# Two wide attention layers: queries projected for three batches at once, and softmax reciprocals spread over partitions by transfers

## The chip, the cores and the metric

The kernel runs on one core of a Trainium2 chip. The metric is the device time of one execution in microseconds (us). Three runs of the kernel before took 2034.56, 2040.13 and 2043.69 us, median 2040.13.

## What is computed

Four cross-attention layers follow one another. All have 16 batches, 100 queries and 361 context rows of width 256, and 16 heads. Layers L0 (with a feed-forward part) and L3 have heads of 16 and are "narrow"; L1 and L2 have heads of 64, so that their projections are 1024 wide, and are "wide". The change touches only the wide ones:

```python
# L1: x -> x + softmax(q k^T) v @ wo
normed = x * rsqrt(mean(x**2, -1) + 1e-6) * norm_w
q, k, v = heads(normed @ wq), heads(ctx @ wk), heads(ctx @ wv)      # 16 heads of 64
x = x + merge(softmax(q @ k.T) @ v) @ wo
# L2: rope on q and k, a key mask, and a layer norm behind the sum
q, k, v = rope(heads(x @ Wq)) / 8, rope(heads(ctx @ Wk)), heads(ctx @ Wv)
s = where(mask, q @ k.T, -1e9)
x = layer_norm(x + merge(softmax(s) @ v) @ Wo, 1e-3) * gamma + beta
```

## The kernel before

Everything is float32. A product that has to be exact enough is made of three float32r matmuls: both factors are split into a high and a low part, and high x high, high x low and low x high are added in PSUM (`product3`, L1358). ACT makes the high part, DVE (or POOL) the low part; so each product of 256 rows is six matmuls and is then taken out of PSUM twice.

`wide_layers` (L1170) runs L1 and L2 as one stream of 32 steps s: 0 to 15 are the batches of L1, 16 to 31 those of L2 ("rope" is `s >= B`). A step has four quarters d, and each quarter treats two head pairs, p = 2d and 2d + 1. The order of PE in a quarter is written out by hand (L1465 and on): the scores of both pairs; `weigh`, the probabilities times V, of the two pairs of the quarter before; the jobs called first (two key products K for the next step); `turn`, six transposes of the probabilities of the first pair; the jobs called mid (values V, the output projection O, and R, below); `turn` of the second pair; the jobs called late (a query product Q, and X). `jobs_at` (L1221) hands the jobs out. All jobs share three PSUM banks in turn: a job waits until the one three places back has been taken out (`begin`).

The scores of a pair lie in two banks. Of the pair that comes first in a quarter DVE copies the turned probabilities out (L1723), of the second ACT does (`unload`, L1591); the second pair's scores of the next quarter wait for that.

Queries: Q(s, p) is the product for head pair p of two batches, s and s + 1, so of 200 columns. X(s) transposes the two batches of x, normed in L1, as input. Step s even makes Q(s + 2, 4 to 7) and step s odd Q(s + 1, 0 to 3), one in each quarter; the tiles QH and QL have 12 places, of which pairs 4 to 7 use two in turn (`q_slot`). In L2 a key or query product also needs rope: DVE shuffles it into SH (L1679), ACT copies it to T32 (L1516), POOL multiplies both by the tables (L1928, L1929), in the next quarter DVE adds them into AC (`join`, L1684), ACT rounds AC to the high part (L1524), and the low part is made by DVE for keys (L1690) and by POOL for queries (L1935), for POOL behind the rotations of that quarter's keys. SH and AC are rings of four, T32 of three. POOL also makes masked tables for the next step at d = 0 (L1909 to L1913).

Reciprocals: the weighed values lie in PSUM with the head's dimension on the partitions and the queries on the columns, but the sums of the exponentials lie with the queries on the partitions. For each half batch (s, r), r = 0 at d = 2 and r = 1 at d = 0 of the next step, DVE takes the reciprocals of eight heads (L1728) and repeats each 64 times into RX (L1732). PE transposes RX in four pieces (job R, L1405), ACT copies the result from PSUM to RB (L1549), and DVE multiplies the weighed values by RB (`scale`, L1739), and later splits off the output's low part (L1744). `weigh` of the next half, at d = 1 for r = 1, waits for `scaled`.

SyncE (SP) issues the transfers of the wide layers in one order: the turned context of each step into the one tile C as soon as DVE has split the one before (L1666, at d = 3), masks, and weights.

Of the kernel before, what the change touches and what calls it, by code (L numbers as in the profile page):

```python
# [4 lines left out]
fp32 = mybir.dt.float32  # L5
# [7 lines left out]
KE = E // 128  # L13
# [23 lines left out]
def build(nc, a, consts, out):  # L37
    stack = ExitStack()
    with stack:
# [30 lines left out]
        strips_dram = nc.dram_tensor("strips", (2, 4, 32, 4, SKE), fp32, kind="Internal").ap()  # L70
        kept_dram = nc.dram_tensor("kept", (B, 2, 128, KE, SK), fp32, kind="Internal").ap()
# [1098 lines left out]
        def wide_layers():  # L1170
# [10 lines left out]
                  "inverse", "repeated", "spread", "scaled", "added", "o_high", "o_low", "wo_high", "wo_low",  # L1181
# [4 lines left out]
            wo2_in = sem("wide_wo2_in")  # L1186
            RAW2 = {"Q": 0, "K": 0, "V": 1}
# [10 lines left out]
            QH, QL = local("QH", [128, 12, 2 * SQ], f32r), local("QL", [128, 12, 2 * SQ], f32r)  # L1198
# [7 lines left out]
            XN = local("XN", [SQ, 2, E])  # L1206
            XTH, XTL = local("XTH", [128, KE, 2 * SQ], f32r), local("XTL", [128, KE, 2 * SQ], f32r)
# [12 lines left out]

            def jobs_at(s, d):  # L1221
# [25 lines left out]
            FIRST = [("K", 0, p) for p in range(4)] + [("X", 0, 0)] + [("K", 0, p) for p in range(4, HP)] + [("Q", 0, p) for p in (4, 5, 6, 7, 0, 1, 2, 3)] + [("X", 2, 0)] + [("V", 0, c) for c in range(3)]  # L1247
# [5 lines left out]
            CHUNKS = [(0, "K", 0, 256), (0, "K", 256, 512), (0, "K", 512, 1024), (0, "Q", 512, 1024), (0, "Q", 0, 512), (0, "V", 0, 512), (0, "V", 512, 1024),  # L1253
                      (1, "Q", 512, 1024), (1, "Q", 0, 512), (1, "K", 0, 256), (1, "K", 256, 512), (1, "V", 0, 512), (1, "K", 512, 768), (1, "K", 768, 1024),
                      (1, "V", 512, 1024)]
            CHUNKS_AT = {(13, 0): [7], (14, 0): [8], (14, 3): [9], (15, 0): [10], (15, 1): [11, 12], (15, 2): [13], (15, 3): [14]}
            CHUNK_AFTER = {7: ("Q", 14, 7), 8: ("Q", 14, 3), 9: ("K", 15, 7), 10: ("K", 15, 7), 11: ("V", 15, 2), 12: ("K", 15, 7), 13: ("K", 15, 7),
                           14: ("V", 15, 5)}

            def q_slot(s, p):  # L1260
                return 4 + p if p >= 4 and s // 2 % 2 else p

            def q_no(s, p):
                return HP * (s // 2) + (p + 4) % 8 + 1
# [32 lines left out]
            def taken(key):  # L1297
                kind, s, n = key
                if kind in "KQ" and rope(s):
                    return Z["copied"], turn_no[key] + 1  # L1300
                return {"K": lambda: (Z["k_low"], HP * s + n + 1), "Q": lambda: (Z["q_low"], q_no(s, n)),
                        "X": lambda: (Z["x_low"], s // 2 + 1), "V": lambda: (Z["v_taken"], 6 * s + n + 1),
                        "R": lambda: (Z["spread"], 2 * s + n + 1), "O": lambda: (Z["added"], s + 1)}[kind]()
# [4 lines left out]
            with nc.Block() as block:  # L1308

                @block.sync  # L1310
                def _(sp):
# [11 lines left out]
                    mask(B + 1)  # L1323
                    for s in range(NS):
                        if s + 1 < NS:
                            sp.wait_ge(Z["c_low"], KE * (s + 1))
                            load_turned_context(sp, s + 1)
                        if s == 0:
# [709 lines left out]
```

## Time and profile before

| | |
|---|---|
| median of 3 runs | 2040.13 us |
| profiled execution | 2039.82 us, span 2038.0 us |
| PE busy | 1936.0 us, 95% |
| DVE busy | 1433.7 us, 70% |
| ACT busy | 1312.6 us, 64% |
| POOL busy | 642.4 us, 32% |
| wide layers | about 455 to 1708 us of the span |

Times are microseconds. PE is TensorE, DVE VectorE, ACT ScalarE, POOL GpSimd. A row of the timeline is: start in the span, duration of the whole group, engine, line, operation, tiles as out<-in, form, how many instructions, and, where the engine was idle before, how long and for whom it waited. Durations of matmuls overlap, as they are pipelined; the difference of two starts is what a piece of work costs PE.

### The profile page before, as it was taken

The numbers are of one execution on the slowest core, as the hardware profiler recorded it, in microseconds if no ns is written. First come the engines' busy times: TensorE is split into PE (matmuls) and PEld (weight loads), VectorE is DVE, ScalarE is ACT, GpSimd is POOL, SyncE is SP. The second block draws the span as 40 slices with busy tenths as digits, with TensorE's granted clock in tenths as the row PEclk, the third lists the DMA queues.
The fourth block names the chain that finished last, engine by engine and source line by source line (L and its number), as shares of the span: only waits on it lengthen the run. The fifth ranks groups of instructions, "written<-read, shape, count | busy, mean of one in ns | idle before, by whom it ended". The sixth has DMA issues, their size and how long they took to land. (4 is left out here: it accounts for less than half of the span.)

```text
span 2038.0 us, 51007 instructions
## 1 busy us (share of the span) xinstructions
PE 1936.0 (95%) x19166; PEld 1683.5 (83%) x19166; DVE 1433.7 (70%) x2779; ACT 1312.6 (64%) x3193; POOL 642.4 (32%) x740
## 2 busy tenths in 40 slices
PE   7799998899999999999999999999999999899998
PEld 6677777898888888888888888888888878787786
DVE  5687786546555555555588888888888885677675
ACT  4576776556656566566576666666666763677775
POOL 3232330000000000000067777877877851000000
PEclk8899999999999999999999999999999998999999
DMA  5444442201000000000001000000000001344442
GB/s 154 150 140 137 134 135 68 91 26 57 14 8 16 9 9 16 9 9 16 29 10 53 11 10 10 18 10 10 17 11 10 9 1 64 119 123 125 129 121 66
DMA packets 72859, 109.65 MB, mean 54 GB/s; under 512 B 7052, under 2 KB 62508, under 8 KB 72620
## 3 DMA queue, kind: packets, MB, share of 16 engines
q1 hardware_dynamic: 72332, 105.88, 17.1%
q8 instruction: 158, 2.59, 0.5%
q14 instruction: 81, 0.66, 0.1%
q10 hardware_dynamic: 288, 0.51, 0.1%
HBM read 69.18 MB, written 37.19 MB: 52 GB/s over the span
## 5 line engine op out<-in xcount | busy, mean ns | idle before, releaser
L1584 ACT ACTIVATE wide_P<-PS,MX 100x361 f32<-100x361 f32 x512 | 280.9, 562 | 126.7 <-DVE MX L1717 126.3
L644 ACT ACTIVATE L_P<-PS,MX 100x361 f32<-100x361 f32 x512 | 252.7, 565 | 129.2 <-DVE MX L774 127.4
L774 DVE TENSOR_REDUCE MX<-PS 100x2 f32<-100x722 f32 x256 | 219.8, 900 | 55.1 <-PE PS L524 54.9
L1717 DVE TENSOR_REDUCE MX<-PS 100x2 f32<-100x722 f32 x256 | 221.2, 900 | 20.2 <-PE PS L1432 19.4
L536 PE MATMUL PP<-CON,L_P 100*128 100x100 f32 x1536 | 181.6, 255 | 27.6 <-DVE L_PT L781 23.1
L536 PEld LDWEIGHTS PP<-CON,L_P 100*128 100x128 f32 x1536 | 149.2, 143 | 48.8 <-ACT L_P L644 34.8
L1439 PE MATMUL PS<-CON,wide_P 100*128 100x100 f32 x1536 | 176.0, 249 | 1.1 <-ACT wide_P L1584 0.6
L1439 PEld LDWEIGHTS PS<-CON,wide_P 100*128 100x128 f32 x1536 | 157.5, 140 | 20.0 <-ACT wide_P L1584 3.1
L1928 POOL TENSOR_TENSOR wide_AC<-wide_T,wide_COSM 128x362 f32<-128x362 f32 x128 | 130.7, 1021 | 125.3 <-ACT wide_T L1516 119.9
L1452 PEld LDWEIGHTS PP<-wide_PT,wide_V 128*64 128x64 f32 (+1 forms) x3072 | 136.1, 136 | 33.1 <-issue 33.1
L1452 PE MATMUL PP<-wide_PT,wide_V 128*64 128x100 f32 (+1 forms) x3072 | 161.2, 253 | 0.6 <-issue 0.5
L1541 ACT ACTIVATE wide_V<-PJ 128x512 f32<-128x512 f32 (+1 forms) x129 | 76.3, 595 | 121.6 <-PE PJ L1358 121.4
L1888 POOL TENSOR_TENSOR VE<-MV 128x2 f32<-128x2 f32 x8 | 1.7, 218 | 477.9 <-DVE MV L1780 477.9
L1929 POOL TENSOR_TENSOR wide_SH<-wide_SH,wide_SINM 128x362 f32<-128x362 f32 x128 | 138.3, 1080 | 0.0
L1358 PE MATMUL PJ<-wide_CTH,wide_WH 128*128 128x362 f32 x338 | 120.0, 355 | 1.9 <-DVE wide_WL L1661 1.0
L1690 DVE TENSOR_TENSOR wide_KL<-wide_AC,wide_KH 128x362 fp32r<-128x362 f32 x128 | 114.2, 932 | 0.0
L1358 PE MATMUL PJ<-wide_CTH,wide_WL 128*128 128x362 f32 x338 | 111.1, 329 | 0.0
L1358 PE MATMUL PJ<-wide_CTL,wide_WH 128*128 128x362 f32 x338 | 111.1, 329 | 0.0
L1358 PE MATMUL PJ<-wide_WH,wide_CTH 128*128 128x512 f32 (+1 forms) x258 | 108.3, 420 | 0.0
L781 DVE COPY L_PT<-PP 128x600 f32<-128x600 f32 x128 | 99.4, 777 | 8.6 <-PE PP L536 3.8
L1584 ACT ACTIVATION_READ_ACCUMULATOR wide_P<-PS,MX 100x1 f32 x512 | 103.7, 203 | 0.0
L1516 ACT ACTIVATE wide_T<-PJ 128x362 f32<-128x362 f32 (+1 forms) x128 | 54.6, 427 | 74.7 <-DVE wide_SH L1679 72.8
(258 smaller groups left out, 5720.2 us busy)
## 6 DMA issues: line engine op xcount, KB each, us to landing
strips<-L_KS SPq DMA_DIRECT2D x256, 90.5 KB
L_KA<-strips SPq DMA_DIRECT2D x64, 362.0 KB, 3.2
C<-ctx_t SPq DMA_DIRECT2D x32, 361.0 KB, 3.1
kept<-L_CTH SPq DMA_DIRECT2D x16, 361.0 KB, 4.7
kept<-L_CTL SPq DMA_DIRECT2D x16, 361.0 KB, 5.3
L_CTH<-kept SPq DMA_DIRECT2D x16, 361.0 KB, 4.2
L_CTL<-kept SPq DMA_DIRECT2D x16, 361.0 KB, 5.0
C<-in_ctx SPq DMA_DIRECT2D x8, 256.0 KB, 3.5
```

The lines of the kernel that those rows point to most:

```text
L536: last = nc.tensor.transpose(PPB[:, n, SQ * t:SQ * t + SQ], P[:, (4 * g + 2 * i + n) % 8, 128 * t:128 * t + 128], ident[0:SQ, 0:SQ])
L644: nc.scalar.activation(P[:, (4 * g + j) % 8, 0:SK], PSB[0:SQ, j, 0:SK], ACT.Exp, bias=MX[:, s % 2, 4 * q + j:4 * q + j + 1], scale=1.0).th ...
L774: nc.vector.tensor_reduce(MX[:, s % 2, 4 * q + 2 * i:4 * q + 2 * i + 2], PSB[0:SQ, 2 * i:2 * i + 2, 0:SK], AX.X, ALU.max, negate=True).the ...
L781: nc.vector.tensor_copy(pt(g)[:, 2 * KV_TILES * SQ:4 * KV_TILES * SQ].rearrange("p (n c) -> p n c", n=2), PPB[:, :, 0:KV_TILES * SQ]).then ...
L1358: last = nc.tensor.matmul(dst, l, r, start=n == 0, stop=n == len(todo) - 1)
L1439: last = nc.tensor.transpose(score_bank(g, i)[:, SQ * t:SQ * t + SQ], P[:, (2 * g + i) % 4, 128 * t:128 * t + 128], ident[0:SQ, 0:SQ])
L1452: last = nc.tensor.matmul(PO[64 * i:64 * i + 64, SQ * at:SQ * at + SQ], V[0:r, 1024 * c + 64 * h:1024 * c + 64 * h + 64], PT[0:r, (2 * g + ...
L1584: nc.scalar.activation(P[:, (2 * g + i) % 4, 0:SK], score_bank(g, i)[0:SQ, 0:SK], ACT.Exp, bias=MX[:, s % 2, h:h + 1], scale=1.0, accum_ou ...
L1690: nc.vector.tensor_tensor(KL[:, p, :], AC[:, r % NB, 0:SKE], KH[:, p, :].bitcast(fp32), ALU.subtract).then_inc(Z["k_low"], 1)
L1717: nc.vector.tensor_reduce(MX[:, s % 2, 2 * p:2 * p + 2], PSB[0:SQ, 2 * (g % 2):2 * (g % 2) + 2, 0:SK], AX.X, ALU.max, negate=True).then_in ...
L1928: nc.gpsimd.tensor_tensor(ac, src, c, ALU.mult)
L1929: nc.gpsimd.tensor_tensor(sh, sh, t, ALU.mult).then_inc(Z["rotated"], 1)
```

## The change

Queries are made for groups: batches (0, 1), (2, 3), (4 to 6), (7 to 9), (10 to 12), (13 to 15) of each layer. A product has 200 or 300 columns, and QH and QL have 8 places with no second one. Q(s0, 0) to Q(s0, 4) are made in the step before the group, one, two, one and one in its quarters, behind the scores that last read the place; Q(s0, 5), Q(s0, 6) at (s0, 0) and Q(s0, 7) at (s0, 1). X is a job for each half of the width, both at d = 3 two steps ahead.

The job R, the tile RX and ACT's copy to RB are gone. DVE takes the reciprocals at d = 1 and d = 3 into RD, transposes it in 32 x 32 blocks into RT, and SP writes RT to a scratch tensor in HBM with four transfers, waits for them, and reads it back into RB with two transfers that repeat each row over 64 partitions. `scale` stays where it was and waits for these. SP's order is now written by quarters, with these steps at d = 1 and 3, at d = 3 behind the context's load. The diff, cut to its core:

```diff
-            QH, QL = local("QH", [128, 12, 2 * SQ], f32r), local("QL", [128, 12, 2 * SQ], f32r)
+            QH, QL = local("QH", [128, 8, 3 * SQ], f32r), local("QL", [128, 8, 3 * SQ], f32r)
-            RX = local("RX", [SQ, H // 2 * 64])
+            RD, RT = local("RD", [128, 32]), local("RT", [128, 32])
...
+            GROUPS = {s0 + l: n for l in (0, B) for s0, n in ((0, 2), (2, 2), (4, 3), (7, 3), (10, 3), (13, 3))}
+            Q_AHEAD, Q_WITHIN = {0: (0,), 1: (1, 2), 2: (3,), 3: (4,)}, {0: (5, 6), 1: (7,)}
...
             def jobs_at(s, d):
-                if s % 2 == 0 and s + 2 < NS:
-                    late.append(("Q", s + 2, 4 + d))
-                if s % 2 and s + 1 < NS:
-                    late.append(("Q", s + 1, d))
-                if s % 2 and d == 3 and s + 3 < NS:
-                    late.append(("X", s + 3, 0))
+                if s + 1 in GROUPS:
+                    late += [("Q", s + 1, p) for p in Q_AHEAD[d]]
+                if s in GROUPS and s > 0:
+                    late += [("Q", s, p) for p in Q_WITHIN.get(d, ())]
+                if d == 3 and s + 2 in GROUPS:
+                    late += [("X", s + 2, k) for k in range(KE)]
-                if d == 0 and s > 0:
-                    mid.append(("R", s - 1, 1))
-                if d == 2 and s < NS:
-                    mid.append(("R", s, 0))
...
                 @block.sync
+                    def reciprocals(s, r):
+                        n = 2 * s + r
+                        sp.wait_ge(Z["inverse_turned"], n + 1)
+                        for b in range(4):
+                            sp.dma_start(recip_dram[n % 2, :, 32 * b:32 * b + 32], RT[32 * b:32 * b + H // 2, :]).then_inc(recip_out, 16)
+                        sp.wait_ge(recip_out, 64 * (n + 1))
+                        if n:
+                            sp.wait_ge(Z["o_low"], n)
+                        for i in range(2):
+                            src = recip_dram[n % 2].rearrange("(t i) q -> i t q", i=2)[i:i + 1, :, 0:SQ]
+                            sp.dma_start(RB[64 * i:64 * i + 64, :, :], src.broadcast_to([64, 4, SQ])).then_inc(recip_in, 16)
...
                     for s in range(NS):
+                        for d in range(4):
...
+                            if d == 3 and s + 3 < NS:
+                                context(s + 3)
+                            if d in (1, 3):
+                                reciprocals(s, d // 2)
...
                 @block.vector
                     def invert(s, r):
                         n = 2 * s + r
                         dve.wait_ge(Z["exped"], HP * (n + 1))
-                        nc.vector.reciprocal(RDEN[:, 0:8], DEN[:, s % 2, 8 * r:8 * r + 8]).then_inc(Z["inverse"], 1)
+                        nc.vector.reciprocal(RD[0:SQ, 0:8], DEN[:, s % 2, 8 * r:8 * r + 8]).then_inc(Z["inverse"], 1)
                         dve.wait_ge(Z["inverse"], n + 1)
                         if n:
-                            dve.wait_ge(Z["made"], job_no["R", (n - 1) // 2, (n - 1) % 2] + 1)
-                        nc.vector.tensor_copy(RX[:, :].rearrange("p (h r) -> p h r", h=H // 2),
-                                              RDEN[:, 0:8].unsqueeze(2).to_broadcast([SQ, H // 2, 64])).then_inc(Z["repeated"], 1)
+                            dve.wait_ge(recip_in, 32 * n)
+                        nc.vector.transpose(RT[:, :], RD[:, :]).then_inc(Z["inverse_turned"], 1)

                     def scale(s, r):
-                        dve.wait_ge(Z["spread"], 2 * s + r + 1)
+                        dve.wait_ge(recip_in, 32 * (2 * s + r + 1))
                         dve.wait_ge(Z["weighed"], HP * s + 4 * r + 4)
...
                     for s, d in SLOTS:
-                        if d == 0 and s:
-                            invert(s - 1, 1)
-                        if d == 2 and s < NS:
-                            invert(s, 0)
                         for key in turns_of(G - 1):
                             join(key)
...
                         for key in turns_of(G - 1):
                             if key[0] == "K":
                                 rotated_low(key)
+                        if d in (1, 3) and s < NS:
+                            invert(s, d // 2)
```

The rest of the diff puts the new counts and column widths into the waits, the instructions for x's moments and POOL's power (three columns, not two), and the order of the first weights.

## Rows read from the trace of the kernel before

**Rows 1.** The page's busy tenths of PE in 40 slices of the span.
```profile
PE   7799998899999999999999999999999999899998
```
**Rows 2.** Timeline, PE: first scores of (1, 0), (15, 0), (16, 0), (30, 0).
```profile
509.55 0.41 PE L1432 MATMUL PS<-wide_KH,wide_QH 64*100 64x362 f32 x2
...
1029.91 0.41 PE L1432 MATMUL PS<-wide_KH,wide_QH 64*100 64x362 f32 x2
...
1069.06 0.41 PE L1429 MATMUL PS<-wide_MNEG,wide_FILL 64*100 64x362 f32 x2
...
1630.87 0.41 PE L1429 MATMUL PS<-wide_MNEG,wide_FILL 64*100 64x362 f32 x2
```
**Rows 3.** Timeline, PE, end of (11, 2): job R, turn, query product; then (11, 3)'s scores.
```profile
907.47 0.51 PE L1405 MATMUL PJ<-CON,wide_RX 100*128 100x100 f32 x4
907.82 0.68 PE L1439 MATMUL PS<-CON,wide_P 100*128 100x100 f32 x6
908.28 0.34 PE L1358 MATMUL PP<-wide_XTH,wide_WH 128*128 128x200 f32 x1
...
909.11 0.41 PE L1432 MATMUL PS<-wide_KH,wide_QH 64*100 64x362 f32 x2
...
909.68 0.33 PE L1432 MATMUL PS<-wide_KH,wide_QH 64*100 64x362 f32 x2
```
**Rows 4.** Groups by line and form, PE: count, busy us, mean ns, idle.
```profile
L1358 PE MATMUL PJ<-wide_CTH,wide_WL 128*128 128x362 f32 x338 | 111.1, 329 | 0.0
...
L1358 PE MATMUL PJ<-wide_WOH,wide_OTL 128*100 128x256 f32 x184 | 51.6, 280 | 0.0
...
L1358 PE MATMUL PJ<-wide_XTH,wide_WL 128*128 128x200 f32 x174 | 47.7, 274 | 0.0
```
**Rows 5.** Timeline, PE and ACT, from (31, 2) to (31, 3), without query products.
```profile
1691.69 0.68 PE L1439 MATMUL PS<-CON,wide_P 100*128 100x100 f32 x6
...
1692.30 0.41 PE L1429 MATMUL PS<-wide_MNEG,wide_FILL 64*100 64x362 f32 x2
1692.43 0.68 ACT L1591 ACTIVATE wide_PT<-PS 128x600 f32<-128x600 f32 x1
...
1693.35 0.41 PE L1429 MATMUL PS<-wide_MNEG,wide_FILL 64*100 64x362 f32 x2 [0.15 <-issue]
```
**Rows 6.** Timeline, PE: scores of (22, 0), (22, 1) first and second, (22, 3).
```profile
1311.12 0.41 PE L1429 MATMUL PS<-wide_MNEG,wide_FILL 64*100 64x362 f32 x2
...
1322.65 0.41 PE L1429 MATMUL PS<-wide_MNEG,wide_FILL 64*100 64x362 f32 x2
...
1324.07 0.41 PE L1429 MATMUL PS<-wide_MNEG,wide_FILL 64*100 64x362 f32 x2 [0.51 <-issue]
...
1342.62 0.41 PE L1429 MATMUL PS<-wide_MNEG,wide_FILL 64*100 64x362 f32 x2
```
**Rows 7.** Timeline, DVE's context split in L1 and L2, POOL's low parts of queries.
```profile
915.39 0.97 DVE L1666 TENSOR_TENSOR wide_CTL<-C,wide_CTH 128x361 fp32r<-128x361 f32 x2
...
1310.15 2.50 DVE L1666 TENSOR_TENSOR wide_CTL<-C,wide_CTH 128x361 fp32r<-128x361 f32 x2
...
1323.44 0.53 POOL L1935 TENSOR_TENSOR wide_QL<-wide_AC,wide_QH 128x200 fp32r<-128x200 f32 x1
...
1344.56 0.53 POOL L1935 TENSOR_TENSOR wide_QL<-wide_AC,wide_QH 128x200 fp32r<-128x200 f32 x1
```
**Rows 8.** Timeline, SP, in L3; then transfers: KB each, median us to landing.
```profile
1734.12 2.14 SPq L302 DMA_DIRECT2D strips<-L_KS  x4
1740.80 0.33 SPq L307 DMA_DIRECT2D L_KA<-strips  x1
...
wide_M<-in_mask SPq DMA_DIRECT2D x16, 45.1 KB, 2.8
```
**Rows 9.** Timeline, DVE, end of L2: last copy to RX and last scale.
```profile
1697.07 0.43 DVE L1732 COPY wide_RX<-RDEN 100x512 f32<-100x512 f32 x1
...
1699.66 0.57 DVE L1739 TENSOR_TENSOR wide_RB<-PP,wide_RB 128x400 f32<-128x400 f32 x1 [2.16 <-ACT wide_RB L1549]
```

More of the change, by code:

```diff
@@ L1218, in rope @@
                 return s >= B
+            GROUPS = {s0 + l: n for l in (0, B) for s0, n in ((0, 2), (2, 2), (4, 3), (7, 3), (10, 3), (13, 3))}
+            STARTS = list(GROUPS)
+            START_OF = {s0 + u: s0 for s0, n in GROUPS.items() for u in range(n)}
+            Q_AHEAD, Q_WITHIN = {0: (0,), 1: (1, 2), 2: (3,), 3: (4,)}, {0: (5, 6), 1: (7,)}
             def jobs_at(s, d):
@@ new lines, in _ @@
+                    context(1)
+                    sp.wait_ge(Z["w_low"], 7)
+                    for m in "QV":
+                        weights(m)
+                    context(2)
+                    for s in range(NS):
+                        for d in range(4):
+                            if (s, d) == (B - 2, 1):
+                                sp.wait_ge(Z["w_low"], 9)
+                                weights("K")
+                            if d == 0 and rope(s) and s + 2 < NS:
+                                sp.wait_ge(Z["m_tables"], s - B + 1)
+                                mask(s + 2)
+                            if (s, d) == (B, 0):
+                                sp.wait_ge(Z["w_low"], len(CHUNKS))
+                                load_weights(sp, "L3")
+                            if (s, d) == (B, 2):
+                                sp.wait_ge(Z["added"], B)
+                                sp.dma_start(WO[:, :].rearrange("p (t n) -> p t n", t=8),
+                                             a["L2_xattn_Wo"].rearrange("(t p) n -> p t n", p=128)).then_inc(wo2_in, 16)
+                            if d == 3 and s + 3 < NS:
+                                context(s + 3)
+                            if d in (1, 3):
+                                reciprocals(s, d // 2)
@@ L1414, in job @@
                     def job(key):
-                        {"K": keys, "V": values, "X": query_turn, "Q": queries, "R": spread, "O": project}[key[0]](key)
+                        {"K": keys, "V": values, "X": query_turn, "Q": queries, "O": project}[key[0]](key)
                     def scores(s, p):
@@ L1431, in scores @@
                             for n, r in halves:
-                                last = nc.tensor.matmul(score_bank(g, n)[0:SQ, 0:SKE], Q_[r, q_slot(s, p), q], K_[r, p, :], start=m == 0 and not rope(s), stop=m == 2)
+                                last = nc.tensor.matmul(score_bank(g, n)[0:SQ, 0:SKE], Q_[r, p, q], K_[r, p, :], start=m == 0 and not rope(s), stop=m == 2)
                         last.then_inc(Z["scored"], 1)
@@ L1542, in values @@
                                              ACT.Copy).then_inc(Z["v_taken"], 1)
-                    def spread(key):
-                        _, s, r = key
-                        act.wait_ge(Z["made"], job_no[key] + 1)
-                        if 2 * s + r:
-                            act.wait_ge(Z["o_low"], 2 * s + r)
-                        nc.scalar.activation(RB[:, :, :].rearrange("p t q -> p (t q)"), bank(key)[:, 0:4 * SQ], ACT.Copy).then_inc(Z["spread"], 1)
                     def output_high(s, r):
```

195 lines of the change are left out of this document (84 added, 111 removed).

## The prediction

> **What bounds the kernel now.** The page's slices show PE busy in nine tenths or more almost throughout; the last slices on the list are a second narrow layer that the change leaves alone [rows 1]. Busy time of pipelined matmuls hides short waits, so I read the wide layers from the starts of PE's instructions. One batch has four quarters (s, d), each of which begins with the scores of a head pair. From (1, 0) to (15, 0), in the plain layer L1, 14 batches take 520.4 us, 37.17 each; from (16, 0) to (30, 0), in the rope layer L2, 561.8 us, 40.13 each [rows 2]. L2's scores have one more step of two matmuls, the mask; one step is a third of 0.57 us [rows 3], and eight pairs make 1.5 us. That leaves 40.13 - 37.17 - 1.5 = 1.45 us of waits in each rope batch, 20 us over 14. In L1 nothing on PE waits: its time is the sum of its starts. So each start of a PE instruction that goes is worth its full price in L1, and in L2 if no wait takes its place.
>
> **The transposes that spread the reciprocals.** One such job begins at 907.47 and the next work at 907.82 [rows 3]: 0.35 us. There are 64, two in each of 32 batches: -22.4 us. With them go an eviction on ACT and a 100x512 copy of 0.43 us on DVE [rows 9]; neither is on PE's path in L1.
>
> **The query products.** A product of 200 columns takes from 908.28 to 909.11, 0.83 us [rows 3]. The means of one matmul are 274 ns at 200 columns, 280 at 256, 329 at 362 [rows 4]; on the line between the last two 300 columns give 300 ns, 26 more, and six make 0.16: 0.99 us for a product of three batches (bounds: 0.87 by the row of 256, 1.25 if it grew with the columns). Before, each of the 120 quarters of batches 0 to 29 has one product: 99.6 us. After, 88 are left there (24 of 200 columns, 64 of 300): 24 x 0.83 + 64 x 0.99 = 83.3, and 22 of them directly follow another and save an end of some 0.1: 81 us. But 54 quarters now have none. What these cost can be seen at the end of L2, where no queries are left: from the last transposes to the scores it is 0.61 us, not 0.46, and the second score waits until 1.05 us after the first, because ACT's unload of the bank (1692.43) was covered by the product [rows 5]. Normal is 0.57 in L1 and 0.57 + 0.19 in L2 [rows 3]. So a bare quarter costs 0.15 + 0.48 in L1 (24 of them) and 0.15 + 0.3 in L2 (19); 11 more have the transposes of x, which cover the unload: 0.15. Together 15.1 + 8.6 + 1.6 = 25.3. After: 106 us, against 99.6: **+7 us**. The regrouping saves products and gives back more. The transposes of x are as many as before (64) in more jobs, DVE's and ACT's work on queries falls; no price.
>
> **L1** alone has 32 of the transpose jobs and 64 of the 120 quarters (13 + 32 products, all 24 bare ones, 6 with x): 57.4 against 53.1 us for its products, so -11.2 + 4.3 = -7 us, if the reciprocals arrive in time.
>
> **The chain of transfers.** In its place per half batch: reciprocal and a 32-column DVE transpose (estimate 0.35 us, from the copy of 0.43 as the nearest row, bounds 0.2 and 1), four small writes issued by SP, a wait for them, two broadcast reads, and only then DVE's scale. SP issues four writes in 2.14 us, about 0.53 each, and the next starts 4.5 us after the last issue ended; a small broadcast read lands 2.8 us after its issue [rows 8]. The new writes are 4 KB, not 362, so I put issues at 0.4 and landing at 3.2 from the last issue; the reads are 512 pieces against the mask's 128: second issue at 0.6, landing 3.3. Sum: 0.1 + 3 x 0.4 + 3.2 + 0.1 + 0.6 + 3.3 = 8.5, and 0.2 for the wake-ups: **8.7 us** (7.0 with 2.5, 2.8 and short issues; 11.6 with 0.53, 5.0 and an estimated 4.1 for the reads). For the second half SP first waits for DVE's context split and issues the context load, 0.5 us more: **9.2 us** from that split's end (7.5 to 12.1). The first half has no context before it, and some 10 us of room by the same count as below (the long (s, 1) stands in it), against 8.7: no price.
>
> The cost is nil where it ends before PE's weigh of (s+1, 1), which waits for scaled; DVE stands at scale meanwhile, with its next shuffle and maxima behind, but the maxima have 1.5 us to spare before the transposes need them. L1: the split ends 7.25 us into (s, 3) [rows 3, 7], 7.6 to 8.1 with the reciprocals; two quarters of some 9.0 (9.3 on average before [rows 2]), scores of 1.6, less 0.6 for scale: 10.8 us of room. 9.2 fits: nothing. L2: the split is 2.50 us long there and ends 1.5 us after (22, 0) has begun [rows 6, 7], 2.1 with the reciprocals and the shorter quarter. (s+1, 0) without waits is some 9.3 + 0.4 for the mask - 0.35: 8.9 us bare, 9.5 with one product, 10.4 with two; with scores of 1.9, 1.5 and 1.5, less 0.6, the room is 8.1, 8.3 and 9.2. So 9.2 costs 1.1, 0.9 and 0: 0.67 a batch, 15 batches: **+10 us** (0 at 7.5; 53 at 12.1).
>
> By the Trainium skill, "DMA: Bandwidth & Descriptors", section "Anatomy of one DMA — SWDGE (gpsimd) path", a transfer has about 2.0 us fixed and the rest by its bytes; an estimate from it is 6.8 us for the second half's chain and no wait at all. The trace disagrees for these queues: 2.8 us for 45 KB [rows 8].
>
> **Single buffers in the rope layer.** A rope query is shuffled by DVE, copied by ACT, rotated by POOL, and POOL takes its low part only in the next quarter, behind both key rotations. Now it hurts once per two batches: at (22, 1) POOL's low is at 1323.44 to 1323.97 and the second score starts at 1324.07, 0.67 late [rows 6, 7]. After, Q(5) is made in (s0, 0) and due in (s0, 2), Q(7) made in (s0, 1) and due in (s0, 3): two quarters, as that one. Q(7): the like low ends at 1345.1, 2.5 after (22, 3) began [rows 6, 7]. With 300 columns 0.3 more; the quarter before is 1.0 shorter (no transpose job, no product), DVE without its copy 0.6 earlier: 3.2 after the start, due at 1.1: 2.1 us late, 0 if POOL gets ahead; I take 1.6. Q(5): (s0, 0) has four turns of the rope ring of four, and mask tables besides, so POOL cannot rotate the next keys until DVE has their forerunners' low parts; counting the quarter through gives 2.3 us late, without the ring nothing; I take 1.7. Per group of three 3.3, of two 2.2 (shorter rotations): 4 x 3.3 + 2 x 2.2 = **17.6 us** (0 to 25). The old waits, 20 us, mostly stood where x's low part, the copy for the spread and the joins met on DVE after (s, 3); I take them as gone (bound: half stay). Net with the chain: 17.6 + 10 - 20.2 = +7.4.
>
> **The end.** Nothing hides the last chain. DVE has the last reciprocals at 1697.07 and scale starts at 1699.66 [rows 9]; after, at 1697.3 + 8.7 = 1706.0: **+6.3 us** (4.6 to 9.2).
>
> **Sum.** -22.4 + 7.0 + 7.4 + 6.3 = -1.7. The profiled execution took 2039.8 us (span 2038.0), 0.3 below the median: 2038.1, and **2038 us** on the scale of the runs.
>
> **Rivals.**
> A, no measurable change, 2038: above. It needs several prices to cancel; its own range is 2028 to 2050.
> B, faster: the rope waits go and none come, since every engine but PE gets less to do there, and the chain is hidden. -22.4 + 7.0 - 20.2 + 6.3 = -29.3: 2011; half of the new waits gives 2024. For it: L1's gain is certain, and stalls counted often overlap. Against it: (22, 1) shows that POOL's low comes late at just this distance.
> C, slower: the chain of the second half ends last before weigh. At 11 us, near the strips' rows, rope batches pay 2.9, 2.7 and 1.8, mean 2.5, x 15 = 37, L1 3, the end 2 more: 2038 + 27 + 3 + 2 = 2070; at 12.1 some 2100. It decides from about 10 us, where 12 more are lost. For it: 4.5 us behind the last strip write [rows 8], and a context load of 361 KB just ahead in the queue. Against it: 4 KB instead of 362.
> The same page of the Trainium skill, in "Specifications", says that transfers in pieces below 512 B are done by read-modify-write; the new pieces are 128 and 400 B, so by it the chain would lean to C. The mask's 361 B pieces landed in 2.8 us [rows 8], which does not show it.
> D, bare quarters don't wait for ACT's unload (something else covers it): 24 x 0.48 + 19 x 0.3 = 17 us less, 2021, counted with B.
>
> **How the numbers follow.** Faster or slower is told from no change at 0.5%, 10 us here. A 0.37; B and D 0.34; C 0.29. A lies within, B and D below 2030, C above 2050. The range of 2012 to 2065 leaves out about one in ten on either side, and holds the ends of the waits counted above except the worst of the chain.
>
> **What would show it.** Per batch in L1: 37.17 to about 36.7, with bare quarters whose second score starts 1.05 us after the first. In L2: second scores of (s0, 2) and (s0, 3) late, released by POOL's QL; weigh of (s+1, 1) released by DVE's scale, and scale by the DMA into RB; SP from the context's issue to landing about 9 us. At the end scale near 9 us after the last reciprocal. I am wrong if SP's chain is under 8 or over 10 us, or if L2's batches stay below 39 or go above 41 us.

## The result and the profile after

The changed kernel takes 2067.3 us, median of four runs (2064.5 to 2069.5), against 2037.7 for the kernel before on the same chip: a ratio of 1.014, 95% interval 1.011 to 1.016. That is slower, by 30 us; "no measurable change" at 2038 was forecast, with a range of 2012 to 2065.

The starts of the same four scores in the profile after, in the order of [rows 2] (timeline, PE: start, us, engine, line, operation, out and in):

```profile
507.02 0.41 PE L1449 MATMUL PS<-wide_KH,wide_QH 64*100 64x362 f32 x2
...
1020.27 0.41 PE L1449 MATMUL PS<-wide_KH,wide_QH 64*100 64x362 f32 x2
...
1059.52 0.41 PE L1446 MATMUL PS<-wide_MNEG,wide_FILL 64*100 64x362 f32 x2
...
1658.75 0.41 PE L1446 MATMUL PS<-wide_MNEG,wide_FILL 64*100 64x362 f32 x2
```

Fourteen batches of the plain layer L1 take 513.25 us for 520.36, -7.1. Fourteen of the rope layer L2 take 599.23 for 561.81, **+37.4**. All else (what lies before (1, 0), between the layers, and after (30, 0)) is -0.7 us together (spans of the profiled executions, 2067.6 and 2038.0 us). So the question is one of the rope layer alone.

Its stretch seen by engine (windows from (16, 0) to (30, 0) of the kernel before, of the one after: length, then busy us and instructions of PE, weight loads, DVE, ACT, POOL; granted clock, DMA share, GB/s):

```profile
1069.06:1630.87 561.81, 548.54 (x4897) 478.84 (x4896) 491.25 (x999) 374.48 (x1018) 435.64 (x474) 1.00 0.06 15
```
```profile
1059.52:1658.75 599.23, 559.23 (x4711) 483.75 (x4710) 482.93 (x966) 366.50 (x970) 435.86 (x441) 0.96 0.10 24
```

Three things are to be seen. PE has 186 instructions fewer and is busy 11 us longer: the granted clock fell from 1.00 to 0.96. The rest of the loss is idle time: 599 - 559 = 40 us against 13. And POOL is as busy as before, with 33 instructions fewer.

Where the time stands is read from PE's starts in one group of three, batches 23 to 25 with the last quarter of 22. I compare each quarter with itself without its waits, from the same trace.

- (22, 3) takes 14.0 us, about 4.0 too many: the second value product waits 2.33 us, and then runs at half the clock.
- (23, 1) 0.75 too many, in the output projection.
- (23, 2) 11.1 us, 3.4 too many, and (23, 3) 12.4 us, 3.3 too many: the second scores wait for QL, and all that follows runs slower for a while.

That is 11.5 us for each group of three, and it repeats in (20, .) and (26, .). The quarter before each group, after: the two POOL rotations and the low parts, then DVE's join, ACT's copy and PE's value product (timelines of POOL, DVE, ACT and PE, then a window over that product):

```profile
1345.98 1.13 POOL L1929 TENSOR_TENSOR wide_AC<-wide_T,wide_COSM 128x362 f32<-128x362 f32 x1 [4.14 <-DVE wide_KL L1699]
...
1348.64 2.58 POOL L1930 TENSOR_TENSOR wide_SH<-wide_SH,wide_SINM 128x362 f32<-128x362 f32 x1
1351.18 1.80 POOL L1937 TENSOR_TENSOR wide_QL<-wide_AC,wide_QH 128x300 fp32r<-128x300 f32 x2
1352.94 0.84 POOL L1929 TENSOR_TENSOR wide_AC<-wide_T,CON 128x300 f32<-128x300 f32 x1
...
1354.58 0.47 DVE L1693 TENSOR_TENSOR wide_AC<-wide_AC,wide_SH 128x300 f32<-128x300 f32 x1 [2.29 <-POOL wide_SH L1930]
...
1355.57 0.47 ACT L1533 ACTIVATE wide_T<-PP 128x362 f32<-128x362 f32 x1 [4.48 <-DVE wide_SH L1688]
...
1356.19 0.77 PE L1384 MATMUL PP<-wide_WH,wide_CTH 128*128 128x512 f32 x1 [2.33 <-ACT wide_T L1533]
```
```profile
1356.00:1359.00 3.00, 2.81 (x7) 2.18 (x8) 2.97 (x6) 2.52 (x7) 2.88 (x3) 0.50 0.02 5
```

Read from the bottom: PE waits for a bank that ACT has not emptied, ACT for DVE's shuffle, DVE stands at the join of the query and cannot shuffle the new keys, and the join waits for POOL. POOL had stood 4.14 us because quarter (22, 1) had made four turned tiles, two of K and two of Q, and the ring of turned tiles has four places: the next key's rotation may not start before DVE has taken KL from the tile four turns back. In its own quarter the query is then behind two keys and two low parts. Behind the wait the granted clock is 0.50, and the product takes 2.70 us from its first start to the turn, where that of (23, 1) takes 1.46.

And the group's first batch, (23, 2) (timelines of POOL and PE, then windows over the same stretch):

```profile
1384.59 1.69 POOL L1937 TENSOR_TENSOR wide_QL<-wide_AC,wide_QH 128x300 fp32r<-128x300 f32 x2
...
1385.59 0.41 PE L1446 MATMUL PS<-wide_MNEG,wide_FILL 64*100 64x362 f32 x2 [1.98 <-issue]
...
1386.42 2.11 PE L1469 MATMUL PP<-wide_PT,wide_V 128*64 128x100 f32 x24
```
```profile
1381.00:1383.00 2.00, 2.00 (x18) 1.72 (x18) 1.60 (x7) 1.38 (x3) 2.00 (x3) 1.00 0.01 2
1383.00:1385.50 2.50, 0.61 (x8) 0.29 (x4) 2.43 (x5) 0.42 (x1) 2.50 (x4) 1.00 0.09 23
1385.50:1388.00 2.50, 2.41 (x30) 2.19 (x32) 1.71 (x4) 1.72 (x6) 2.50 (x3) 0.72 0.25 66
1388.00:1391.00 3.00, 3.00 (x19) 2.76 (x16) 1.32 (x4) 1.06 (x5) 1.01 (x1) 0.66 0.00 0
1391.00:1393.50 2.50, 2.50 (x19) 2.06 (x18) 2.07 (x5) 1.79 (x5) 1.75 (x2) 1.00 0.00 0
```

PE waited 1.98 us for QL, which POOL began only at 1384.59, behind two rotations. Behind the wait the granted clock is 0.72 and 0.66, a mix of its two levels of 2.4 and 1.2 GHz: the weighing takes 2.0 us to the next start for 1.19 elsewhere, the key products 2.8 for 2.1. Here a wait of 2 us costs 3.4.

The chain of transfers, at the end of L2 where nothing else runs (timelines of DVE and SP; and the page's row of the reads: KB each, median us to landing):

```profile
1720.95 0.21 DVE L1742 STREAM_TRANSPOSE wide_RT<-wide_RD 128x32 f32<-128x32 f32 x1
1721.19 1.29 SPq L1339 DMA_DIRECT2D recip<-wide_RT  x4
1723.37 1.24 SPq L1345 DMA_DIRECT2D wide_RB<-recip  x2
...
1726.80 0.57 DVE L1748 TENSOR_TENSOR wide_RB<-PP,wide_RB 128x400 f32<-128x400 f32 x1 [5.64 <-DMA wide_RB<-recip]
```
```profile
wide_RB<-recip SPq DMA_DIRECT2D x128, 100.0 KB, 2.8
```

5.85 us from transpose to scale, not 8.7. The four writes issue in 1.29, the wait for them is 0.9, not 3.2, and the reads land in 2.8. In all 64 halves DVE's scale waited 9.7 us for these transfers, 5.6 of them here, and no wait of PE ends with that scale.

### The profile page after: what moved, and what is told of

Read it like the earlier page. It is cut to its first block and busy times, and to the rows that moved or that the text cites. A ratio compares the mean times of both kernels' runs of the same rounds, so it can differ in the third digit from the quotient of the medians.

```text
span 2067.6 us, 50143 instructions
## 1 busy us (share of the span) xinstructions
PE 1928.9 (93%) x18718; PEld 1664.5 (81%) x18718; DVE 1410.1 (68%) x2724; ACT 1287.5 (62%) x3089; POOL 622.6 (30%) x684
## 5 line engine op out<-in xcount | busy, mean ns | idle before, releaser
L1469 PEld LDWEIGHTS PP<-wide_PT,wide_V 128*64 128x64 f32 (+1 forms) x3072 | 144.7, 143 | 34.2 <-issue 34.2
L1469 PE MATMUL PP<-wide_PT,wide_V 128*64 128x100 f32 (+1 forms) x3072 | 171.0, 263 | 0.7 <-issue 0.6
L1384 PE MATMUL PJ<-wide_CTH,wide_WH 128*128 128x362 f32 x348 | 125.2, 360 | 2.0 <-DVE wide_WL L1670 1.0
L1384 PE MATMUL PJ<-wide_CTL,wide_WH 128*128 128x362 f32 x348 | 115.3, 331 | 0.0
L1693 DVE TENSOR_TENSOR wide_AC<-wide_AC,wide_SH 128x362 f32<-128x362 f32 (+2 forms) x176 | 90.1, 547 | 36.2 <-POOL wide_SH L1930 36.2
L1533 ACT ACTIVATE wide_T<-PJ 128x362 f32<-128x362 f32 (+2 forms) x117 | 52.6, 452 | 83.2 <-DVE wide_SH L1688 83.0
```

The lines of the kernel that those rows point to most:

```text
L1384: last = nc.tensor.matmul(dst, l, r, start=n == 0, stop=n == len(todo) - 1)
L1469: last = nc.tensor.matmul(PO[64 * i:64 * i + 64, SQ * at:SQ * at + SQ], V[0:r, 1024 * c + 64 * h:1024 * c + 64 * h + 64], PT[0:r, (2 * g + ...
```

## Experiments

The theory after the result was: the transfers are a gain, and the rope layer lost by the queries' lateness on POOL, at two places (the ring, the order of the low parts), with the clock's fall on top. The rival: the transfers did it, by their chain or their traffic. "L1" and "L2" below are the 14 batches from (1, 0) and from (16, 0), from PE's starts; "idle" is PE's idle time in L2, and "low clock" the time in L2 for which the granted clock was at its lower level, read from narrow windows. Ratios are to the kernel before on the same chip, with 95% intervals (its median was 2037.7 to 2041.7). "Threes" are groups of three, "pairs" groups of two. The code shown is abridged. The last four columns are of one profiled execution each; those of threes_turned and threes_ring6 took 7.7 and 6.4 us more than the medians of their kernels.

| kernel | us | ratio | L1 | L2 | idle | low clock |
|---|---|---|---|---|---|---|
| before | 2037.7 | 1 | 520.4 | 561.8 | 13.3 | 0 |
| after | 2067.3 | 1.014 (1.011 to 1.016) | 513.3 | 599.2 | 40.0 | 51 |
| pairs_transfers | 2035.7 | 0.998 (0.996 to 1.000) | 510.3 | 568.3 | 18.9 | 31 |
| threes_turned | 2058.7 | 1.009 (1.006 to 1.013) | 513.3 | 596.6 | 37.9 | 24 |
| threes_ring6 | 2047.3 | 1.004 (1.002 to 1.006) | 513.2 | 576.5 | 34.4 | 10 |
| threes_lows_first | 2041.0 | 0.999 (0.998 to 1.001) | 513.3 | 574.2 | 28.0 | 24 |
| pairs_lows_first | 2015.3 | 0.988 (0.986 to 0.990) | 510.3 | 546.8 | 9.8 | 0 |
| threes_filled | 2054.6 | 1.007 (1.005 to 1.009) | 513.2 | 584.4 | 23.7 | 14 |
| threes_lows_ring6 | 2041.4 | 1.000 (0.999 to 1.001) | 513.2 | 568.7 | 27.7 | 10 |
| threes_earlier_lows_ring6 | 2031.5 | 0.995 (0.993 to 0.998) | 515.4 | 556.1 | 18.5 | 3 |
| before_lows_first | 2030.1 | 0.995 (0.994 to 0.997) | 520.4 | 555.0 | 5.8 | 0 |
| pairs_low_between | 2007.8 | 0.985 (0.983 to 0.988) | 510.3 | 539.9 | 6.0 | 0 |
| pairs_lows_ring6 | 2011.8 | 0.987 (0.984 to 0.989) | 510.3 | 545.8 | 9.1 | 0 |
| threes_writes_twice | 2066.8 | 1.014 (1.011 to 1.017) | 513.3 | 597.0 | 40.6 | 44 |
| threes_earlier_between | 2027.0 | 0.994 (0.992 to 0.997) | 515.4 | 553.0 | 16.8 | 0 |
| pairs_between_ring6 | 2009.5 | 0.986 (0.984 to 0.988) | 510.3 | 536.8 | 3.1 | 0 |

The filler products of threes_filled count as busy, so its idle time can't be compared. But that run gives a price for the clock: 37 us less at the lower level made L2 14.9 us shorter, 0.4 us for each. With it the loss of the change in L2 adds up (an estimate for the clock): 26.7 us more idle, 51 x 0.4 = 20 for the clock, 28 transpose jobs of 0.35 less, 9.8; together 37, as measured. "By the clock's price" below means this 0.4.

**One part alone: transfers with groups of two.**

```
...                                            (in the kernel before; queries untouched)
-                    mid.append(("R", s - 1, 1))   and ("R", s, 0), RX, the copy and ACT's eviction
+                        if d in (1, 3) and s < NS:
+                            invert(s, d // 2)     # reciprocal, transpose; SP: four writes, two reads
```


> The kernel before with one part of the change alone: the reciprocals go through DRAM by transfers and no longer through transposes on TensorE; queries stay in groups of two with twelve buffers. If the transfers are a plain gain (theory: their chain never ends a wait of TensorE, and the loss of the whole change is all in the queries' buffers), the 64 R steps of 0.35 us go, 22.4 us, and the last projection's wait gives 3.3 back: 2038 - 22.4 + 3.3 = about 2019 us (2010 to 2026), with the second wide layer near 551 us (562 - 11). If instead the transfers cost the wide layers time (rival: SyncE's queue or the DMA traffic, 14 to 22 GB/s in the profile after against 9 to 13 before, delays contexts and rotations in the rope layer), this kernel is at 2038 or above and its rope layer is over 562 us.

L1 came out as summed: 520.4 - 510.3 = 10.1 for 28 jobs, 0.36 each. L2 did not: 568.3, over the rival's threshold for the layer, though the whole, 2035.7, is under its 2038. The theory failed as it stood, and the trace says why; the rival's cause is not to be seen in it either. The quarter (22, 1) takes 14.9 us where it took 11.6 (timelines of POOL and PE, then windows):

```profile
1304.60 2.71 POOL L1909 TENSOR_TENSOR wide_COSM<-CON,wide_MNEG 128x362 f32<-128x362 f32 x1
...
1313.18 0.53 POOL L1933 TENSOR_TENSOR wide_QL<-wide_AC,wide_QH 128x200 fp32r<-128x200 f32 x1
...
1313.82 0.41 PE L1438 MATMUL PS<-wide_MNEG,wide_FILL 64*100 64x362 f32 x2 [2.29 <-issue]
```
```profile
1313.00:1315.00 2.00, 1.18 (x16) 0.96 (x18) 0.24 (x1) 0.71 (x4) 1.78 (x4) 1.00 0.00 0
1315.00:1317.00 2.00, 2.00 (x24) 1.76 (x21) 2.00 (x5) 1.29 (x5) 0.00 (x0) 0.54 0.00 0
1317.00:1320.00 3.00, 3.00 (x19) 2.97 (x18) 1.21 (x6) 0.77 (x2) 0.20 (x1) 0.74 0.00 0
```

In the kernel before PE waited 0.51 us for the like QL [rows 6, 7]. POOL's path to it, with mask tables and two key rotations ahead of the low part, is as long as before: from the start of (22, 0) to the low part it is 12.3 us in the kernel before and 12.6 here. But PE takes 10.0 us for (22, 0), where it took 11.5. Of these 1.5 us the transposes themselves are 0.35; for 1.12 they had waited for a bank (timeline, PE, the kernel before):

```profile
1319.44 0.54 PE L1405 MATMUL PP<-CON,wide_RX 100*128 100x100 f32 x4 [1.12 <-ACT wide_T L1516]
```

So PE now arrives at QL earlier by the transposes and by their wait, stands 2.3 us, and then runs at 0.54 of its clock. No wait of PE ended with a transfer of reciprocals. Over the layer: 5.6 us more idle, and 12 us for the clock by its price, against the 10 us that were taken out.

**The other part alone in L2: transposes again, groups of three kept.**

```
+                if d == 0 and s > B:      mid.append(("R", s - 1, 1))
+                if d == 2 and B <= s < NS: mid.append(("R", s, 0))
-                            if d in (1, 3):
+                            if d in (1, 3) and s < B:
                                 reciprocals(s, d // 2)
```


> The changed kernel with the reciprocals of the second wide layer alone sent through transposes on TensorE again; groups of three in single buffers stay, and so do the transfers in the first wide layer. Theory (the queries' buffers alone make the loss): the rope layer keeps its waits of 12 us for each group of three and gets 32 R steps of 0.35 us, 11.2 us, in part inside those waits, and the tail's 3.3 us go: 2067 + 4 to 11 - 3 = 2068 to 2075 us. Rival (the transfers make the loss in the rope layer): it comes back to 562 + 3 us there and the whole to 2045 us or less.

L2 is 596.6: with 9.8 us of transposes put back it is 2.6 shorter than after. They are not hidden inside waits, since PE's idle time is 37.9 us for 40.0. What pays for them is the clock, 24 us at the lower level for 51, which is 11 us by its price. PE has 15 waits above 1.5 us in L2, against 16 after, but the clock fell at 7 of them, against 15. So the groups of three keep their waits without the transfers, and the rival's 2045 is out. Why the clock fell less often here is open. My 2068 to 2075 missed as well (2058.7): it didn't count the clock.

**The ring.**

```
...
+            ring_slot = [r % NB if r < deep else (r - deep) % 6 for r in range(len(turn_no))]
+            # places 4 and 5 of SH and AC lie in the unused part of W_RAW; deep = turn of K(17, 4)
```


> The changed kernel with six places in place of four in the ring of rotated tiles (SH and AC), from the second batch of the rope layer on; all else as it is. Theory: part of the loss is that a quarter with four turned tiles (two K, two Q) fills the ring of four, so that GpSimd's next K rotation waits 4.1 us for KL and VectorE's join then holds up the copies behind it. With six places the long V of the quarter before each group's first batch (6.67 us for 2.87) goes, 5 times 3.8 to 5.4 us, and the K rotation's 2.7 us wait in the group's first batch too: 2040 to 2050 us. Rival (only the late queries of single buffers count, distance of two quarters): within 5 us of 2067.

2047.3 us is as expected. POOL's wait for KL is gone, and (22, 3) takes 11.4 us for 14.0 (timelines of POOL and PE; compare 4.14 and 2.33):

```profile
1342.02 0.97 POOL L1938 TENSOR_TENSOR wide_AC<-wide_T,wide_COSM 128x362 f32<-128x362 f32 x1 [3.00 <-ACT wide_T L1542]
...
1352.25 0.47 PE L1393 MATMUL PP<-wide_WH,wide_CTH 128*128 128x512 f32 x1 [1.22 <-ACT wide_T L1542]
```

Yet of the 22.8 us by which L2 is shorter only 5.6 are PE's idle time. The greater part, 16 us by its price, is the clock, which stood at its lower level for 10 us and not 51.

**POOL's order.**

```
                         for key in turns_of(4 * s + d):
                             if key[0] == "K":
-                                rotate(key)                # ahead of rotated_low
+                                rotate(key)                # behind rotated_low
```


> The changed kernel with GpSimd's order turned: in each quarter it takes the low parts of the quarter before's queries ahead of this quarter's K rotations, not behind them. Theory: the second scores of (first batch, third and fourth quarter) wait for QL, 2.0 and 1.9 us plus the slow clock behind them (3.9 and 3.5 us together with it), since QL stands behind the K rotation on GpSimd; with the low part first these go, 5 times about 7 us, and the K rotations come perhaps 1.5 us later, with slack: 2030 to 2050 us. If the ring of four holds GpSimd up anyway, or the rotation becomes late in turn, within 5 us of 2067 or above.

2041.0 us is as expected, and L2 is 25 us shorter: 12.0 of idle time, and 11 by the clock's price. In (23, 2) the second score is on time (1.49 us for both). What was left there moved half a quarter on, to (23, 3): 3.1 us for its scores.

**The same order with groups of two, and in the kernel before.**

> Groups of two with transfers (2035.7 us), and GpSimd's low parts of the queries ahead of its K rotations. In the run with transfers alone the first wide layer gained 10.1 us, as the sum wants, but the rope layer took 568.3 us for 561.8: at each even batch's second quarter the second score now waits for QL (at 1313.82 us [2.29 idle]), which GpSimd makes at 1313.18 behind the mask's tables and two K rotations, and the granted clock is 0.54 behind it; the quarter takes 14.9 to 16.1 us for 11.6. Theory (time taken from TensorE ahead of a GpSimd deadline comes back as wait and slow clock): with the low part ahead of the rotations QL comes 3.4 us earlier, 7 quarters times 4 to 5 us go: 2035.7 - 28 to 35 = 2001 to 2010 us. Rival (the transfers themselves, or VectorE, bound the rope layer): within 6 us of 2036.

> The kernel before with GpSimd's low parts of the queries ahead of its K rotations, nothing else. It asks how much of the transfers' gain was hidden by that deadline. Theory: in the kernel before the transposes' time is itself part of what covers the deadline, so the wait for QL is small there (second score 2.26 us for 1.5 at each even batch's second quarter, 7 times), and only this and part of the 1.3 us wait in the quarter before go: 2041 - 5 to 14 = 2027 to 2036 us. Then the transfers are worth 2031 - 2015 = 12 to 21 us once the deadline is out of the way, for 5 to 6 with it. If this kernel came to 2015 too, the transfers would be worth nothing in the rope layer.

(22, 1) takes 10.9 us for 14.9, L2 546.8 for 568.3; the total missed the forecast by 5 us, since the rotations now come late and (s, 3) pays 0.5 us. In the kernel before the order alone gives 10 us, as expected (2030.1). On that footing the transfers are worth 0.995 against 0.988, 15 us, of which L2 gives 8.2 (555.0 to 546.8), where they had cost 6.5 without it. With the new order the clock stays at its upper level through the layer.

**The clock's share.**

```
+                        if rope(s) and s > B and (s - START_OF[s], p) in ((0, 5), (0, 7)):
+                            pe.wait_ge(*unloaded(g - 2))
+                            keep_busy(score_bank(g, 0), 7)
                         pe.wait_ge(Z["q_low"], q_no(s, p))
```


> The changed kernel with seven filler products on TensorE in the wait for QL in the third and fourth quarter of each rope group's first batch (from batch 18 on); they are needless work and only keep the engine busy. Theory: of 3.9 and 3.5 us a wait costs there, about 1.6 is the granted clock of 0.54 to 0.7 behind the wait (weighing 2.0 to 2.2 us for 1.19). With the wait filled these go, 10 times 1.2 to 1.6 us: 2067 - 12 to 16 = 2051 to 2056 us, with the weighing at 1.19 there. Rival (the slow stretch has another cause, or the filler is itself as long as what it saves): within 4 us of 2067.

A ratio of 1.007 for 1.014, 13 us, as expected (2054.6), and the row that decides is the weighing behind the filler (timeline, PE):

```profile
1379.61 1.83 PE L89 MATMUL PS<-CON 128*128 128x128 f32 x14
1381.62 0.41 PE L1449 MATMUL PS<-wide_MNEG,wide_FILL 64*100 64x362 f32 x2 [0.18 <-POOL wide_QL L1940]
...
1382.45 1.26 PE L1472 MATMUL PP<-wide_PT,wide_V 128*64 128x100 f32 x24
```

1.26 us for 2.11. The scores are still as late (3.67 us for 3.71), so this is the clock's part by itself: L2 is 14.9 us shorter, with ten waits filled. The long value products of (22, 3) were not filled, and there the clock still fell.

**Both repairs, and queries made earlier.**

> The changed kernel with both repairs: low parts ahead of the K rotations (2041.0 us alone) and six places in the ring (2047.3 us alone). If the two waits are separate, both gains add, 2067 - 26 - 20 = 2021 us (2017 to 2027); if they are one chain of GpSimd's lateness seen at two places, the second repair adds little: 2033 to 2040 us.

```
-            Q_AHEAD, Q_WITHIN = {0: (0,), 1: (1, 2), 2: (3,), 3: (4,)}, {0: (5, 6), 1: (7,)}
+            Q_AHEAD, Q_WITHIN = {0: (0, 1), 1: (2,), 2: (3, 4), 3: (5,)}, {0: (6, 7)}
```


> The same with both repairs and the queries made earlier: Q(0) and Q(1) in the quarter that frees the first, then Q(2); Q(3) and Q(4); Q(5); and Q(6), Q(7) in the group's first quarter, so that no query has fewer than three quarters from its product to its scores. Theory (the deadline of two quarters is what is left of the loss): no wait for QL is left in the group's first batch, 2010 to 2020 us. Rival (quarters with four turned tiles cost by themselves, and there are now four of them for three in each group): no faster than the kernel with both repairs.

The two repairs do not add: 568.7 in L2, for 576.5 and 574.2 alone, and 2041.4 in all, near the forecast of one chain (2033 to 2040) and far from that of two (2021). PE's idle time is 27.7 us, for 28.0 with the order alone. So they are in the main two views of one lateness of POOL. Earlier queries take 12.5 us more out of L2, but at 2031.5 us the forecast of 2010 to 2020 was missed: in (23, 2) and (23, 3) the second scores wait no longer than for the unload of their bank (1.87 us for both, as in every quarter without queries). What stays is (22, 3), 13.8 us: three quarters of each group have four turned tiles now, where two had them (the expectation miscounted them).

**The best order on POOL, and the ring with groups of two.**

```
+                        for key in keys_now[:1]:  rotate(key)
+                        for key in lows:          rotated_low(key)
+                        for key in keys_now[1:]:  rotate(key)
```


> Groups of two with transfers, and the low part of the query between the two K rotations of the quarter. In the kernel with the low part first (2015.3 us) GpSimd stands up to 4.0 us idle for QH with turned tiles ready behind it, and its rotations then come late: the value products of batch's fourth and even first quarters take 3.4 for 2.9 us. Theory: with one rotation ahead of the low part that wait is filled, the low part still comes 1.7 us earlier than at first, and up to 28 times 0.5 us go: 2002 to 2014 us. If 1.7 us are not enough for QL at the second score, the waits of the kernel with transfers alone come back: up to 2035 us.

> Groups of two with transfers, low parts first, and six places in the ring. With one query in each quarter no quarter has four turned tiles. Theory (the ring of four binds only where there are four): the same as with four places, 2011 to 2019 us. Rival (the ring binds everywhere in the rope layer): 2000 to 2010 us.

Between the rotations is best, and as expected: 2007.8 us, **1.5% faster than the kernel before** and 2.8% than the changed one. The wait for QL at (22, 1) is down to this (timelines of POOL and PE):

```profile
1300.02 0.54 POOL L1933 TENSOR_TENSOR wide_QL<-wide_AC,wide_QH 128x200 fp32r<-128x200 f32 x1
...
1300.66 0.41 PE L1438 MATMUL PS<-wide_MNEG,wide_FILL 64*100 64x362 f32 x2 [0.61 <-issue]
```

With one query in each quarter six places took 0.9 us out of L2 (2011.8 us, as expected), for 22.8 in the changed kernel: the ring of four matters where a quarter has four turned tiles.

**The chain made longer.**

```
-                        for b in range(4):
-                            sp.dma_start(recip_dram[n % 2, ...
+                        for z, b in [(n % 2, b) for b in range(4)] + [(2 + n % 2, b) for b in range(4)]:
+                            sp.dma_start(recip_dram[z, ...
```


> The changed kernel in which SyncE writes each half's reciprocals to DRAM twice (the second time to a place that nobody reads), so that the chain from the transpose to the data in RB is longer by four issues of 0.3 us, 1.3 us. Theory (the chain ends no wait of TensorE in the wide layers, except at the very end): 2067 + 1 to 2 us. Rival of the prediction (the chain of transfers is what the change lost by): 64 halves times up to 1.3 us, 2090 us or above.

The writes take 2.64 us to issue for 1.29, and the last scale waits 7.02 us for 5.64. L2 takes 597.0 us and the whole 2066.8, 1.014 of before, as the changed kernel does. DVE now waits 29.1 us in all for these transfers, where it waited 9.7, and still none of it reaches PE: its idle time in L2 is 40.6 us for 40.0. The prediction's rival of a chain that ends last is out.

**What is left of the threes.**

> Groups of three, transfers, queries made earlier, six places in the ring, and the low parts between the quarter's two K rotations in place of ahead of both (2031.5 us with them ahead). Theory: what is left of the threes' loss is GpSimd's order in the quarters with four turned tiles (value products 5.8 and 4.9 us for 2.9 in the last quarter before a group), and it shrinks as for groups of two (2015.3 to 2007.8 us): 2018 to 2027 us, still 7 us or more behind groups of two, since the bare and the double quarters of the first wide layer and the four-tile quarters stay. Rival (groups of three are as good as groups of two once no query is late): 2012 us or less.

> Groups of two with transfers, the low part between the two K rotations, and six places in the ring. What is left there is the wait for QL at each even batch's second quarter (second score 2.34 us for 1.5, 7 times 0.8 us), which the ring does not touch; the ring gave 3 us with the low part first. 2002 to 2010 us; if the quarter's copies were held by the ring, 2002; if not, 2008 as without it.

Under the same order, the same ring and with transfers, groups of three take 515.4 and 553.0 us, groups of two 510.3 and 536.8. The whole times, 2027.0 and 2009.5 us, lie at the upper ends of their forecasts. Some 21 us stay with the grouping (17 by the whole times), and with the earlier queries that the threes have here: in L1 bare quarters cost more than the saved products; in L2 (22, 3) with 11.0 and (23, 0) with 11.4 us still wait behind the four-tile quarters. How these 16 us of L2 divide was not tried. Six places beside the order between take 3.1 us out of L2, which the whole time doesn't show (0.986 for 0.985).

## Why the prediction was wrong

- **Transposes, -22.4: right as a price, wrong as a gain in L2.** 0.36 us each in L1. In the rope layer the same removal alone made the layer 6.5 us longer (568.3 for 561.8), because PE came earlier to a deadline that POOL sets and the clock fell behind the wait. The prediction priced what a start of PE costs "if no wait takes its place", and did not ask it of this part.
- **Query products and bare quarters, +7.0: nearly right.** A product of 300 columns takes 1.00 us (0.99 was put), a bare quarter's scores 1.59 and its last transposes 0.61 in L1 (0.43 + 0.15 over the usual, for 0.48 + 0.15). The regrouping costs 3.0 us in L1's fourteen batches (513.3 - 510.3), for 4.3 in all sixteen.
- **L1, -7: right**, -7.1 in fourteen of the sixteen batches.
- **Chain of transfers, 8.7 and 9.2 us, +10: wrong.** 5.85 us at the end of L2, no wait of PE. The term failed at the wait for the writes: 0.9 us, where 3.2 was taken from the strips' rows [rows 8], which are writes of another size. The estimate by the Trainium skill, "DMA: Bandwidth & Descriptors", section "Anatomy of one DMA — SWDGE (gpsimd) path", 6.8 us with the context's issue and no wait, was the closer one, though that section is on another engine's queue. The read-modify-write of pieces below 512 B, in "Specifications" of the same page of the Trainium skill, shows in no row: the reads land in 2.8 us, as the mask did.
- **The end, +6.3: mis-sized** with the chain. Scale comes 5.85 us after the transpose where it came 2.59 after the copy [rows 9], +3.3.
- **Single buffers in the rope layer, 17.6 us: this step failed.** The fourteen batches hold 40.0 us of idle time and, by its price, some 20 us of slow clock, where I had put 17.6 and 10 in all. The places (s0, 2) and (s0, 3) were right, and at 2 us each so was the wait itself. Three things were missing. First the clock, which the sum put at nothing: filling ten waits gave back 14.9 us in L2. Second the ring's effect at the end of the step before the group: the four tiles of (s0-1, 1) stop POOL in (s0-1, 2), and (s0-1, 3) then takes 4 us more, the wait and the clock behind it. I had looked for the ring in the group's first quarter only. Third, I gave POOL's lateness as an event in a quarter, when it is a debt carried along: each repair alone takes 23 to 25 us out of L2, both 31.
- **Old rope waits, -20.2: gone where they stood**, (22, 0) takes 10.0 us for 11.5 with the transfers alone, but not gained: PE then stands for QL in the next quarter.
- The condition written for being wrong, L2's batches above 41 us, was met: 599.23 / 14 = 42.8. So was "chain under 8". Rival C named nearly the right time, 2070, with the wrong mechanism, which is luck.

## What to carry to other kernels

When an engine's work is cut, look first for the next deadline that another engine sets in order: the time may only become a wait there, and on TensorE a wait of some 2 us cost up to 4.6 here, since the granted clock mostly fell behind it. Price a shortened buffer distance by walking the slowest engine's queue in order, with what stands ahead of the item and what debt it brings from the quarter before. And a cheap change of order in that queue is worth trying before the change that needs it: here it was worth 10 us alone, and it raised what the transfers gave from 5 us to 15. And where a repair shortens a stage, read its idle time and its granted clock apart: of the ring's 22.8 us only 5.6 were waits.

## What was not expected of the hardware

The granted clock fell behind waits of only 1.6 to 2.4 us on an engine that was busy nearly throughout before, and was back at 1.00 within 5 us of the end of the waits at 1313.82 and 1385.59. In the kernel before, where no wait in L2 is above 1.13 us, it stayed at 1.00. It does not fall behind every such wait, and that shows its price with nothing else changed: the same quarter of three groups of two, (20, 1), (22, 1) and (24, 1) of pairs_transfers, each with a wait of 2.29 us and nearly the same busy time on DVE, ACT and POOL (windows):

```profile
1231.58:1244.98 13.40, 11.11 (x102) 9.97 (x102) 8.44 (x19) 6.34 (x18) 8.58 (x11) 1.00 0.01 2
1310.62:1325.51 14.89, 12.60 (x101) 11.36 (x101) 8.40 (x19) 6.34 (x18) 8.58 (x11) 0.89 0.00 0
1391.17:1407.28 16.11, 13.82 (x102) 12.39 (x102) 8.25 (x19) 6.33 (x18) 8.57 (x11) 0.79 0.01 1
```

Against 11.6 us in the kernel before, the wait by itself costs 1.8 us, and the clock nothing, 1.5 or 2.7 more. What decides between the three is open.

POOL's product of 128x362 took 2.58 us at 1348.64 and 0.83 at 1347.07 in the kernel after. Beside the long one DVE had two operations with two inputs in SBUF (timeline, DVE, the kernel after):

```profile
1349.39 0.56 DVE L1753 TENSOR_TENSOR wide_OTL<-wide_RB,wide_OTH 128x400 fp32r<-128x400 f32 x1
1349.87 0.53 DVE L1693 TENSOR_TENSOR wide_AC<-wide_AC,wide_SH 128x362 f32<-128x362 f32 x1
```

The mask table of 2.71 us in the first experiment also stood beside three such joins. By the Trainium skill, "GPSIMD Engine Reference", section "Specifications", GpSimd shares its SBUF interfaces with VectorE and contends with its instructions of two SBUF inputs. The traces agree so far: in the kernel before the same table (L1911) took 0.83 us in the seven batches of L2 in which no such DVE operation ran beside it, and 2.2 in the seven in which three joins did. But the overlap is only 1.0 of the 1.75 us above, and no run here took the two apart. If it is so, DVE's joins and low parts themselves make POOL late; that is not shown.
